# Moving a normalization behind a projection, splitting the expert scaling, interleaving the router, and a bf16 copy of x1 through memory

## The reference, cut to what matters

```python
q, v = x @ Wq.T, x @ Wv.T
ret  = scan(state = lam*state + v_t)           # over the tokens, one lam per head
out  = layernorm(q * ret) * gamma + beta       # over D: "LN1"
out  = out * silu(x @ Wg.T)
x1   = layernorm(x + out @ Wo.T)               # "LN2"
w    = top2 of sigmoid(x1 @ Wgate.T), divided by their sum
g    = silu(x1 @ W1.T) * (x1 @ W3.T) * w[:, :, None]     # per expert
y    = layernorm(x1 + sum_e g_e @ W2_e.T)      # "LN3"
```

## Time and profile before

| | |
|---|---|
| median of three runs | 4537.64 us (4533.3 to 4540.9) |
| the profiled execution, its own time | 4534.37 us |
| its span, first to last instruction of the slowest core | 4532.8 us |
| spans of the 8 cores | 4520.5 to 4532.8 us |
| mean granted TensorE clock | 0.92 to 0.93 of full speed |
| TensorE (matmul) busy | 3948.2 us, 87% of the span |
| VectorE, ScalarE, GpSimd busy | 1177.1, 351.7, 352.1 us |

### The profile page before, as it was taken

How to read it: one execution, slowest core, us unless ns; L and a number is a source line. 1 busy time by engine, 2 the same in 40 slices (tenths; PEclk the granted TensorE clock), 3 DMA queues, 4 the chain that set the end, 5 groups by cost and what they waited for, 6 DMA issues and landing times.

```text
span 4532.8 us, 46515 instructions; the slowest of 8 cores (4520.5 to 4532.8 us)
## 1 busy us (share of the span) xinstructions
PE 3948.2 (87%) x17449; PEld 1700.5 (38%) x17449; DVE 1177.1 (26%) x2023; ACT 351.7 (8%) x622; POOL 352.1 (8%) x666
## 2 busy tenths in 40 slices
PE   5599887299999999999959978719999999999994
PEld 1243332044444444444414433204444444444441
DVE  0122532511212211212263243251221121121216
ACT  0002111000000000000010211100000000000001
POOL 2100000100000000000100000010000000000000
PEclk6699899599999999999979989959999999999997
DMA  9843254444744444444554435544464444444441
GB/s 156 142 75 61 47 112 121 58 71 72 145 78 70 75 70 74 77 73 70 80 134 71 70 44 104 131 58 69 71 142 75 70 77 73 70 78 71 71 79 74
DMA packets 132168, 380.59 MB, mean 84 GB/s; under 512 B 15216, under 2 KB 23408, under 8 KB 131952
## 3 DMA queue, kind: packets, MB, share of 16 engines
q0 software_dynamic: 94608, 310.45, 42.7%
q1 hardware_dynamic: 28128, 50.39, 3.7%
q10 hardware_dynamic: 9216, 16.78, 1.0%
HBM read 654.42 MB, written 33.55 MB: 152 GB/s over the span
## 4 chain that ended last, share of the span: by engine, by line
PE 83%; DVE 6%; DMA 5%; issue 3%; ACT 2%; POOL 0%; DVEq 0%; ACTq 0%; PEldq 0%; POOLq 0%; SPq 0%
PE ps L943 20%; PE ps L1015 20%; PE ps L961 20%; PE ps L622 5%; PE ps L693 5%; PE ps L482 5%; PE ps L553 5%; DMA wring<-xpre 3%; DMA xcS<-x1hbm 1%; DVE x1tS L706 1%; DVE rstdR L409 1%; DVE ot2S L1104 1%; PE ps L920 1%; DMA wring<-wvT 1%; PE ps L423 1%
## 5 line engine op out<-in xcount | busy, mean ns | idle before, releaser
L943 PE MATMUL ps<-xnS,wring 128*128 128x512 bf16 x4096 | 939.2, 389 | 0.0
L961 PE MATMUL ps<-xnS,wring 128*128 128x512 bf16 x4096 | 904.9, 379 | 0.0
L1015 PE MATMUL ps<-gbufS,wring 128*128 128x512 bf16 x4096 | 886.4, 379 | 0.0
L943 PEld LDWEIGHTS ps<-xnS,wring 128*128 128x128 bf16 x4096 | 407.7, 100 | 526.0 <-issue 66.1
L1015 PEld LDWEIGHTS ps<-gbufS,wring 128*128 128x128 bf16 x4096 | 400.2, 98 | 484.9 <-issue 3.5
L961 PEld LDWEIGHTS ps<-xnS,wring 128*128 128x128 bf16 x4096 | 400.7, 98 | 483.3
L984 DVE TENSOR_TENSOR gtmpS<-ps,sh1S 128x512 bf16<-128x512 f32 x256 | 176.0, 687 | 1470.6 <-PE ps L961 1470.6
L977 ACT ACTIVATE sh1S<-ps 128x512 bf16<-128x512 f32 x256 | 138.9, 595 | 2366.9 <-PE ps L943 2366.9
L482 PE MATMUL ps<-xnS,wring 128*128 128x512 bf16 x1024 | 231.7, 385 | 52.8 <-ACT vS L509 36.5
L1040 DVE SCALAR_TENSOR_TENSOR x2S<-ps,x2S 128x512 f32<-128x512 f32 x192 | 132.7, 691 | 517.5 <-PE ps L1015 517.5
L622 PE MATMUL ps<-xnS,wring 128*128 128x512 bf16 x1024 | 238.6, 388 | 31.3 <-ACT ygS L635 31.1
(11 more groups left out here) (129 smaller groups left out, 1470.4 us busy)
## 6 DMA issues: line engine op xcount, KB each, us to landing
wring<-w1T POOLq DMA_DIRECT2D x128, 512.0 KB, 5.7
wring<-w3T POOLq DMA_DIRECT2D x128, 512.0 KB, 5.7
wring<-w2T POOLq DMA_DIRECT2D x128, 512.0 KB, 6.0
wring<-xpre POOLq DMA_DIRECT2D x48, 512.0 KB, 10.0
xf32S<-xfm SPq DMA_DIRECT2D x64, 256.0 KB, 6.8
wring<-wvT POOLq DMA_DIRECT2D x32, 512.0 KB, 5.6
wring<-wqT POOLq DMA_DIRECT2D x32, 512.0 KB, 5.5
wring<-wgT POOLq DMA_DIRECT2D x32, 512.0 KB, 6.1
```

Of the source, the lines that this page charges most:

```text
L943: g1 = pr.step("pe", lambda en, kt=kt, c=c, slot=slot1: en.matmul(out=psS[c][:, 0:CW], lhsT=wringS[slot][:, kt * P:(kt + 1) * P], rhs=x1nS ...
L961: g3 = pr.step("pe", lambda en, kt=kt, c=c, slot=slot3: en.matmul(out=psS[2 + c][:, 0:CW], lhsT=wringS[slot][:, kt * P:(kt + 1) * P], rhs= ...
L1015: grp = pr.step("pe", lambda en, k=k, c=c, slot=slot2: en.matmul(out=psS[4 + c][:, 0:CW], lhsT=wringS[slot][:, k * P:(k + 1) * P], rhs=gbu ...
```

## The change

Five edits, all within a half:

- LN1's `ln_rows_bcast` is emitted behind the g projection instead of ahead of it, and the g projection uses banks 6 and 7.
- In the Wo stage a second write of each x1tS tile, with a cast to bf16, goes to a new tensor x1bhbm from GpSimd's queue. LN2's read-back takes it from there, from SyncE's queue, in 16 pieces of 1024 columns through a ring of two.
- The router's loop over token tiles becomes a function, which is called ahead of each ft of the first expert; it uses banks 6 and 7.
- L984's product goes straight to gbufS, and the broadcast of an expert's weights and the product with them (L993) are emitted behind all eight ft of the expert.
- gtmpS goes; sh1S has four buffers instead of two, and LN3's statistics use them for both.

```diff
-            bt1 = ln_rows_bcast(st_sum + st_sq, 0, 2, 4, 5)
             ...
             for mt in range(NH):
                 slot, wb, tld = load_wcol(wg_d[mt]...)
-                            out=psS[c][:, 0:CW],          # L622
+                            out=psS[6 + c][:, 0:CW],
...
                 yg_sil[mt] = sil
+
+            bt1 = ln_rows_bcast(st_sum + st_sq, 0, 2, 4, 5)
...
                     x1w_toks[(mt, c)] = tw
+                    twb = pr.dma("pool", lambda en, mt=mt, c=c, x1slot=x1slot: en.dma_start(
+                        out=x1bhbm[mt * P:(mt + 1) * P, hoff + c * CW:hoff + (c + 1) * CW],
+                        in_=x1tS[:, x1slot * CW:(x1slot + 1) * CW]),
+                        deps=[t_add], sem=f"dA{x1slot}")
+                    x1buf.read(twb)
...
             for kt in range(KT):
-                for c in range(NCW):
-                    xcslot, xcbuf = xcR.next()
-                    trb = pr.dma("pool", ... in_=x1hbm[..., hoff + c * CW:hoff + (c + 1) * CW]),
-                        deps=t_x1w_all + xcbuf.begin_write(), sem=f"dC{xcslot}")
+                xcslot, xcbuf = xcR.next()
+                trb = pr.dma("sp", ... in_=x1bhbm[kt * P:(kt + 1) * P, hoff:hoff + TH]),
+                    deps=t_x1bw_all + xcbuf.begin_write(), sem=f"dC{xcslot}")
...
-            for tt in range(TT):
+            def emit_router_tt(tt):
...
                 for ei in range(2):
                     e = 2 * pp + ei
-                    (for each c: L920 matmul to bank 6, L927 copy to ewbS)
+                    pend = {}
                     for ft in range(FT):
+                        if first_expert and ft < TT:
+                            emit_router_tt(ft)
                         (W1 group, W3 group)
                         for c in range(NCW):
                             (Silu to sh1S)
-                            (product of bank 2 + c and sh1S to gtmpS; product of ewbS and gtmpS to gbufS)
+                            (product of bank 2 + c and sh1S to gbufS)
+                            pend[(ft, c)] = tg1
+                    (for each c: L920 matmul to bank 6, L927 copy to ewbS)
+                    for ft in range(FT):
+                        for c in range(NCW):
+                            (product of ewbS and gbufS to gbufS)
```

More of the change, by code:

```diff
@@ L35, in __init__ @@
         names += [f"dG{i}" for i in range(4)] + [f"dR{i}" for i in range(4)]
-        names += [f"dW{i}" for i in range(4)] + [f"dA{i}" for i in range(2)]
+        names += [f"dW{i}" for i in range(4)] + [f"dA{i}" for i in range(4)]
         names += [f"dC{i}" for i in range(4)]
@@ L220, in build @@
     x1R = Ring(3)
[L221 to L222 removed]
+    sh1R = Ring(4)
     otR = Ring(4)
@@ L757, in emit_half @@
             t_x1w_all = [(f"dW{k}", pr.counts[f"dW{k}"]) for k in range(4)]
+            t_x1bw_all = [(f"dA{k}", pr.counts[f"dA{k}"]) for k in range(4)]
             bt2 = ln_rows_bcast(st2_sum + st2_sq, 4, 6, 2, 3)
@@ L900, in emit_half @@
                     deps=[tn2, te1])
[L901 removed]
+                d7 = psB[7].begin_write()
                 ttb = pr.tick("pe", lambda en: en.transpose(
[L903 to L905 removed]
+                    out=psS[7][0:E, 0:P], in_=ewtS[:, 0:E],
+                    identity=identf[:, :]), deps=[te2, t_id] + d7)
+                psB[7].wrote(ttb)
                 tee = pr.tick("dve", lambda en, tt=tt: en.tensor_copy(
[L907 removed]
+                    out=ewTf[0:E, tt * P:(tt + 1) * P], in_=psS[7][0:E, 0:P]),
                     deps=[ttb])
[L909 removed]
+                psB[7].read(tee)
                 ew_done.append(tee)
+            first_expert = True
             for pp in range(4):
@@ L982, in emit_half @@
                             shbuf.wrote(ts1)
-                            gtslot, gtbuf = gtR.next()
-                            tg1 = pr.tick("dve", lambda en, c=c, shslot=shslot, gtslot=gtslot: en.tensor_tensor(
-                                out=gtmpS[:, gtslot * CW:(gtslot + 1) * CW],
+                            tg1 = pr.tick("dve", lambda en, ei=ei, ft=ft, c=c, shslot=shslot: en.tensor_tensor(
+                                out=gbufS[:, (ei * FT + ft) * TH + c * CW:(ei * FT + ft) * TH + (c + 1) * CW],
                                 in0=psS[2 + c][:, 0:CW],
@@ new lines, in emit_half @@
+                    if first_expert:
+                        for tt in range(FT, TT):
+                            emit_router_tt(tt)
+                        first_expert = False
+                    ewb_done = []
+                    dw = ewbB.begin_write()
+                    for c in range(NCW):
+                        d6 = psB[6].begin_write()
+                        tb = pr.tick("pe", lambda en, e=e, c=c: en.matmul(
+                            out=psS[6][:, 0:CW],
+                            lhsT=e8f[:, e * P:(e + 1) * P],
+                            rhs=ewTf[0:E, c * CW:(c + 1) * CW],
+                            start=True, stop=True),
+                            deps=ew_done[-1:] + [t_e8] + d6)
+                        psB[6].wrote(tb)
+                        te = pr.tick("dve", lambda en, c=c: en.tensor_copy(
+                            out=ewbS[:, c * CW:(c + 1) * CW],
+                            in_=psS[6][:, 0:CW]), deps=[tb] + dw)
+                        psB[6].read(te)
+                        ewb_done.append(te)
+                        dw = []
@@ L994, in emit_half @@
+                    ewbB.wrote(ewb_done[-1])
+                    for ft in range(FT):
+                        gbb = gbufB[ei][ft]
+                        gd = None
+                        for c in range(NCW):
+                            tg1 = pend[(ft, c)]
+                            gd = pr.tick("dve", lambda en, ei=ei, ft=ft, c=c: en.tensor_tensor(
                                 out=gbufS[:, (ei * FT + ft) * TH + c * CW:(ei * FT + ft) * TH + (c + 1) * CW],
                                 in0=ewbS[:, c * CW:(c + 1) * CW],
-                                in1=gtmpS[:, gtslot * CW:(gtslot + 1) * CW],
+                                in1=gbufS[:, (ei * FT + ft) * TH + c * CW:(ei * FT + ft) * TH + (c + 1) * CW],
@@ L1059, in emit_half @@
                     x2b = x2B[ht][c]
-                    cbslot, cbbuf = gtR.next()
+                    cbslot, cbbuf = sh1R.next()
                     tc_ = pr.tick("dve", lambda en, ht=ht, c=c, cbslot=cbslot: en.tensor_copy(
-                        out=gtmpS[:, cbslot * CW:(cbslot + 1) * CW],
+                        out=sh1S[:, cbslot * CW:(cbslot + 1) * CW],
                         in_=x2S[:, ht * TH + c * CW:ht * TH + (c + 1) * CW]),
@@ L1136, in build @@
         [f"dG{i}" for i in range(4)] + [f"dR{i}" for i in range(4)] + \
-        [f"dW{i}" for i in range(4)] + [f"dA{i}" for i in range(2)] + \
+        [f"dW{i}" for i in range(4)] + [f"dA{i}" for i in range(4)] + \
         [f"dC{i}" for i in range(4)] + [f"out{i}" for i in range(4)]
```

68 lines of the change are left out of this document (24 added, 44 removed).

## The result

The changed kernel is slower: the ratio to the kernel before is 1.109, with a 95% interval of 1.106 to 1.113. Its executions took 5033.4, 5036.3, 5040.9 and 5046.7 us. The forecast was 4987 (4885 to 5100), slower. Three fifths of the loss lie in the Wo stage, where it is 50 us larger than forecast; everything else came within a few microseconds.

What follows compares the result with a forecast made beforehand. TensorE's matmuls fill 87% of the span, so time is lost where it stands still. 128 + 247 - 13 + 2 x (14 + 30) = +450 us on 4534.4 gives 4984, as median 4987; 8-in-10 range 4885 to 5100.

Steps and rivals of the forecast that it cites:

- LN1 behind g: LN1 after the g projection: 94.9 us from g's end to the first Wo group's end; +64 us a half, +128 in all.
- The second write: Wo stage: weight loads held behind waiting writes in GpSimd's queue, +247 us over 30 steps (bounds +208 to +304).
- the step of 19.55 us: Wo stage: forecast length of one step, from one group's end to the next, instead of 11.3 us.
- Rival (c): Wo stage: writes don't hold back loads, as GpSimd hands on a waiting transfer; no +247, 4740 us; chance 0.06.
- Rival (a): Wo stage: TensorE stays cold, 13.7 us a group instead of 9.4; +127, 5114 us; chance 0.12.
- rival (b): Wo stage: the weight load lands as the page's formula says, 4.4 us; kernel 4900 us; chance 0.08.
- Read-back: LN2's read-back of x1 from SyncE: 2.2 us a tile, 35 us instead of 41.6; -6.6 a half, -13 in all.
- rival (e): LN2's read-back is slow, a load taking near 7.8 us; +64 + 13, kernel 5064 us; chance 0.08.
- Router: Router between the ft: interleaved but not covered, 57.6 us against 43.6; +14 us a half (bounds +2 and +20).
- Rival (d): TensorE passes a waiting step, so LN1 broadcast and router chains are covered; faster, about 4457 us; chance 0.02.
- Deferred scaling: Ahead of W2: chunk 0 ends 15.4 us behind the last W3 group, before 3.6; 4 x 13.8 = +55 us a half.

Runs made afterwards that it cites:

- p_ln1: Kernel before with LN1's rows and broadcasts alone emitted behind the g projection, g in banks 6 and 7: 4659.9 and 4665.1 us against 4532.
- b_ln1: Kernel before with LN1 spread, its broadcasts behind the 2nd and 4th group of g: 4492.5 to 4495.5 us, ratio 0.990.
- p_wait: Kernel before, each Wo group's weight load waiting for the last residual add of the group before, no second write: ratio 1.055, +249 to +256 us.
- u_ahead: The whole change, each Wo load emitted two groups earlier: no ratio; four cores' spans 4736.1 to 4749.1 us against the changed kernel's 5014.7 to 5045.1.
- b_cover: Kernel before with router interleaved and scaling deferred, but the transpose back behind the W1 group: ratio 0.995, 4508.5 to 4514.8 us.
- b_experts: b_cover with scaling deferred for the first expert only, later broadcasts behind an expert's first W1 group: ratio 0.968; 4378.3, 4406.5 and 4407.1 us.
- the three parts alone: Kernel before with one part each: LN1 +128 to +133 us, second write and read-back +288 to +306, router and deferred scaling +92 to +100.
- b_spcopy: Kernel before with the bf16 copy of x1 alone, written from cbS by SyncE's queue, read-back from SyncE: ratio 0.999 (0.995 to 1.003).
- p_bf16: Kernel before with the second write from GpSimd's queue and the read-back from SyncE's alone: 4820.5 and 4838.3 us, +288 to +306.

## Why the prediction was right, and where it was off

**LN1 behind g.** Right in mechanism and size: +127.5 against +128; p_ln1 shows it alone, and b_ln1 shows that it was the place behind all of g and not the move behind the start of g: with the broadcasts between g's groups its executions take 4492.5 to 4495.5 us, some 40 less than the kernel before. b_ln1 moves the broadcasts in TensorE's order and the square roots in ScalarE's at once; what either would cost alone no run shows.

**The second write.** Right in mechanism, too small in size: +297 against +247. The term that was mis-sized is the step of 19.55 us; it measured 20.88, which is 40 us in 30 steps. Its parts, each the mean of the 30 steps of core 3: the load issues 3.3 us behind the group's end instead of 2.7, because GpSimd issues half a microsecond after the add ends, which no row that I had used shows; TensorE starts 8.5 us after the issue instead of 7.4; the group takes 9.1 us instead of 9.4. The middle part was the largest error. The load itself landed in 8.1 us at the median, not 7.3, since the two cast writes ahead of it cost 1.1 us (8.1 against 7.0 in p_wait) and not the 0.4 that I let them, and a few loads took longer (up to 10.2 us to TensorE's start). Another 10 us are an error of reading: the second window of the earlier trace rows ends at 2945.20, while the last Wo group there ended at 2934.96, so 30 steps of the kernel before took 328.9 us and not 339.2. These two make up the 50 us. Rival (c), that the writes don't hold back the loads, is refuted by the order of issue in the step above and by u_ahead. Rival (a), a cold clock for whole groups, did not come: groups took 8.4 to 10.0 us and not 13.7, and the stage had a granted clock of 0.73, between the two levels of 0.5 and 1. A weight load of 1.05 MB landed in 8.1 us here and in 7.0 in p_wait. By the fit of the Trainium skill ("DMA: Bandwidth & Descriptors", "Anatomy of one DMA — SWDGE (gpsimd) path") it would be an estimated 4.4 us. The trace disagrees; by that page the step would have been forecast shorter yet, and rival (b) was refuted.

**Read-back.** -16.1 against -13. The read-back itself, from its first to its last operation, is 13.9 us shorter: the load from SyncE lands in 2.7 us (3.0 taken), and rival (e), 7.8, did not come. LN2's square root needed no table load of 1.28 us in either half, since no Silu lies between it and LN1's any more, which I had not counted: from the last Wo group to the first operation of the read-back 25.7 us pass instead of 26.9, in each half.

**Router.** 5.5 to 5.9 us from group to group, 5.6 forecast. b_cover shows the reason: the same chain leaves no idle time once the transpose back stands behind the W1 group. Rival (d), that TensorE passes a waiting step, is refuted here and at LN1.

**Deferred scaling.** 15.9 us behind the W3 group against 15.4 forecast. b_cover and b_experts together give it its price with the broadcasts: 125 us less from the router to LN3 in the two traces, where 122 were forecast for b_experts.

The sum held because the steps lie one behind the other on TensorE's path, which the three parts alone show. No large errors cancelled: the one large miss is the Wo step, and it stands in the total, 50 us above the forecast.

## What to carry to other kernels

Where each engine works off a list in order, an operation is as exposed as the latest thing that stands ahead of it there: a broadcast, a transpose or a store that waits must be emitted behind work that covers its wait, and never ahead of a prefetch. Splitting a stage "to overlap it" moves nothing if both ends of its chain stay on one side of the covering work. When a window is measured, check its ends against the first and the last instruction.

## What the runs showed of the hardware

GpSimd issued a transfer 0.5 us after the VectorE operation that it had waited for had ended (p_wait: add end 673.28, issue 673.82); SyncE did so within 0.1 us (in b_spcopy the add ends at 702.05, and SyncE issues at 702.12). A weight load behind two cast writes of 128 KB in the same queue landed in 8.1 us (8.0 in p_bf16), and in 7.0 without them (p_wait); these are medians, of runs in which a load is issued only when the one before it has long landed. A read of 256 KB of bf16 from SyncE's queue landed in 2.7 us, where 128 KB with a cast from GpSimd's queue had taken 4.1. A Wo group takes 7.1 us when it runs warm. Behind the short pause of a step of the kernel before (some 3.5 us) it took 7.1 or some 8.1 to 8.8 us; behind the 12 us of the changed kernel's step, 8.4 to 10.0.
